# Twelve instead of six shared steps ahead of the expert blocks in the last sparse layer

## The reference, cut to what matters

```
x = x + 0.5 * L3_ffn(layernorm(x))
x = x + L3_attn(layernorm(x))
x = x + 0.5 * L3_ffn(layernorm(x))

L3_ffn(x):                                     # 8 experts of 176, two per token; shared part of 704
    probs  = softmax(x @ W_router.T)           # [T, 8]
    rw,sel = top_k(probs, 2)
    sh     = (silu(x@Ws_gate) * (x@Ws_up)) @ Ws_down
    shared = sh * sigmoid(x @ W_sgate.T)
    eo[e]  = (silu(x@We_gate[e]) * (x@We_up[e])) @ We_down[e]
    return shared + sum_e combine[:, e] * eo[e]
```

## Time and profile before

| | |
|---|---|
| median of 3 runs | 3719.99 us (3718.23 to 3720.12) |
| the profiled execution, its own time | 3711.44 us |
| its span, first to last instruction | 3709.6 us |
| mean granted TensorE clock | 0.895 of full |
| PE busy / DVE busy / ACT busy / POOL busy | 3038.5 / 2194.1 / 1489.1 / 1115.9 us |

### The profile page before, as it was taken

How to read it: one execution, slowest core, us unless ns; L and a number is a source line. 1 busy time by engine, 2 the same in 40 slices (tenths; PEclk the granted TensorE clock), 3 DMA queues, 4 the chain that set the end, 5 groups by cost and what they waited for, 6 DMA issues and landing times.

```text
span 3709.6 us, 56721 instructions
## 1 busy us (share of the span) xinstructions
PE 3038.5 (82%) x19164; PEld 2581.3 (70%) x19164; DVE 2194.1 (59%) x5486; ACT 1489.1 (40%) x3661; POOL 1115.9 (30%) x1085
## 2 busy tenths in 40 slices
PE   4597999999999955889479796948888685986698
PEld 2476888888888834769458594836666574975597
DVE  3644555555555546556473667657778667655664
ACT  2124443444444321233532344437677344424342
POOL 2002222222222220054350544541111455431543
PEclk8798999999999967999779997859899887998899
DMA  2002111111111110033110243520000263311232
GB/s 77 1 0 92 64 48 63 47 63 47 65 45 66 47 46 0 7 95 111 46 34 0 88 124 94 135 74 2 1 1 1 70 160 115 105 56 46 85 107 74
DMA packets 115095, 222.71 MB, mean 60 GB/s; under 512 B 17313, under 2 KB 66945, under 8 KB 110273
## 3 DMA queue, kind: packets, MB, share of 16 engines
q1 hardware_dynamic: 80754, 149.30, 12.5%
q0 software_dynamic: 21472, 58.36, 6.1%
q10 hardware_dynamic: 12672, 12.58, 1.0%
HBM read 172.74 MB, written 47.85 MB: 59 GB/s over the span
## 4 chain that ended last, share of the span: by engine, by line
PE 37%; issue 29%; DVE 16%; POOL 8%; ACT 5%; DMA 4%; SPq 0%; DVEq 0%; ACTq 0%; POOLq 0%
PE bank L502 9%; PE bank L504 9%; PE bank L503 9%; POOL HWL L1737 3%; POOL YG L1498 2%; POOL KL L1753 2%; PE bank L1081 2%; PE bank L1997 1%; DVE ST L528 1%; PE bank L2013 1%; ACT XN L552 1%; PE bank L1103 1%; DMA YG<-dyo,POSI 1%; DMA MXG<-dxn,IDX 1%; DVE SG L749 1%
## 5 line engine op out<-in xcount | busy, mean ns | idle before, releaser
L1488 POOL DMA_INDIRECT MXG<-dxn,IDX x250 | 237.5, 950 | 319.2 <-PE bank L1081 163.8
L1753 POOL TENSOR_TENSOR QL<-QG,QH 128x512 fp32r<-128x512 f32 x64 | 83.0, 1296 | 729.7 <-ACT QH L1645 729.7
L1498 POOL DMA_INDIRECT YG<-dyo,POSI x192 | 190.1, 990 | 218.2 <-DMA dyo<-YS 110.7
L1683 DVE TENSOR_TENSOR X<-bank,X 128x512 f32<-128x512 f32 x128 | 82.5, 686 | 226.9 <-PE bank L504 226.9
L622 PE MATMUL bank<-TAB,XN 128*128 128x128 f32 x320 | 72.8, 385 | 168.1 <-ACT XN L552 127.7
L1480 POOL TENSOR_TENSOR MWL<-RAW,MWH 128x608 fp32r<-128x608 f32 (+2 forms) x118 | 182.1, 1553 | 79.2 <-ACT MWH L1184 73.0
L1478 POOL CAST MWH<-RAW 128x608 fp32r<-128x608 f32 (+2 forms) x78 | 55.0, 705 | 467.6 <-DVE X L884 369.1
L622 PEld LDWEIGHTS bank<-TAB,XN 128*128 128x128 f32 x320 | 52.2, 196 | 181.7 <-ACT XN L552 114.3
L502 PE MATMUL bank<-MWH,GH 128*128 x500 | 173.9, 348 | 0.0
L2174 DVE COPY PT<-bank 128x384 f32<-128x384 f32 x256 | 131.8, 551 | 64.0 <-PE bank L1997 55.3
L502 PE MATMUL bank<-MWH,SHH 128*128 128x256 f32 x352 | 110.1, 313 | 72.2 <-DVE SHL L1357 57.9
(11 more groups left out here) (439 smaller groups left out, 11201.2 us busy)
## 6 DMA issues: line engine op xcount, KB each, us to landing
dyo<-YS SPq DMA_DIRECT2D x250, 128.0 KB
RAW<-in_wheads SPq DMA_DIRECT2D x68, 320.0 KB, 3.0
RAW<-in_eL SPq DMA_DIRECT2D x64, 304.0 KB, 2.9
BB<-dgates SPq DMA_DIRECT2D x17, 1024.0 KB, 4.5
GB<-dgates SPq DMA_DIRECT2D x17, 1024.0 KB, 6.5
dxn<-XN ACTq DMA_DIRECT2D x16, 512.0 KB, 4.3
RAW<-in_eL SPq DMA_DIRECT2D x32, 256.0 KB, 2.7
RAW<-in_sL SPq DMA_DIRECT2D x18, 384.0 KB, 3.9
```

Source lines behind the costliest of these rows:

```text
L1488: nc.gpsimd.indirect_dma_start(MXG[:, n % XGS, :], None, dxn, bass.IndirectOffsetOnAxis(ap=IDX[:, b:b + 1], axis=0)).then_inc(x_in[n % XGS ...
L1498: nc.gpsimd.indirect_dma_start(YG[:, i % YGS, :], None, dyo[0:m.blocks * P, :], bass.IndirectOffsetOnAxis(ap=POSI[:, c * NT + t:c * NT + t ...
L1753: nc.gpsimd.tensor_tensor(lo[:, :], src[:, :], f32(hi[:, :]), ALU.subtract).then_inc(qk_ready, 1)
```

## The change

`pre` of the layer goes from 1 to 2, so `early` = 12 and `late` = 12 in stages A and B; everything derived from them moves too (`pieces_by`, `added_in`, `slot_of`). The four DVE chunks stay at steps 2 to 5. The products of chunks 2 and 3 (`moe_inverse`) move from behind the loop into steps 6 and 7, and `moe_index` from step 5 to step 7. The two other sparse layers have `early` = 6 before and after, and their order is the same as before.

```diff
-    'L3': Sparse(E=L3_E, F=L3_I, J=6, pre=1, act=ACT.Silu, gated=True, router=3),
+    'L3': Sparse(E=L3_E, F=L3_I, J=6, pre=2, act=ACT.Silu, gated=True, router=3),
@@ moe_tensor
                 if s == 5:
                     moe_inverse(pe, st, 1)
+                if s in (6, 7):
+                    moe_inverse(pe, st, s - 4)
                 if s:
                     shared_down(pe, st, s - 1)
-            moe_inverse(pe, st, 2)
+            if m.early == 6:
+                moe_inverse(pe, st, 2)
             shared_down(pe, st, m.early - 1)
-            moe_inverse(pe, st, 3)
+            if m.early == 6:
+                moe_inverse(pe, st, 3)
             warm(24, 1)
@@ moe_vector
                 if s == 5:
                     moe_hot(dve, st, 3)
+                if s == (5 if m.early == 6 else 7):
                     moe_index(dve, st)
             shared_add(dve, st, m.pre - 1)
```

## The result

The changed kernel takes 3711.32 us (median of 20 runs, 3695.37 to 3727.34), the kernel before 3722.66 us (20 runs, 3707.52 to 3734.78). The ratio is 0.9963, with a 95% interval of 0.9948 to 0.9979: 0.37% or some 13.8 us faster. The profiled execution took 3698.85 us, with a span of 3697.0 and a granted clock of 0.894, against 3711.44, 3709.6 and 0.895 before: 12.6 us less of both.

A forecast was written before the change was run, and what follows sets the result against it. PE was taken to set the pace in the late steps, DVE during the routing. A +12.5 - 24.7 = -12.2 and B +20.9 - 24.7 = -3.8, together -16.0 from 3720.0: 3704 us, range 3697 to 3714.

The forecast's parts named there:

- Stage B, early: Stage B up to its first turn: six more early steps and bare warm matmuls bring that turn 23.3 us later.
- The give-back by rows that lie ready: Start of B's block pipeline: gathered rows already there give back 2.4 us (bounds 0 and 3).
- The late phase: Late steps of both stages: six steps fewer, -25.4 us, plus 0.7 of combine waits, so -24.7 each.
- Rival 2: Late phases: the gathers set the pace, four us more in each stage, total 3712 us; chance 0.08.
- Stage A, early: Stage A up to its first turn: DVE sooner but POOL ending last, so that turn comes 12.5 us later.
- The relief of DVE: A's routing: fewer POOL pieces collide with DVE, so SHL of step 5 comes 8.7 us sooner.
- the price of the pieces that stay: A's routing: each of six POOL pieces still beside DVE's work ahead of SHL of step 5 costs 1.0 us.
- From there PE goes at its pace: Early steps behind the down of step 6, both stages: PE waits for nothing, 4.23 us per step.
- rival 4: Moved early steps run at half clock, up to 4.2 us more each; all twelve give 3754 us; chance 0.05.
- Rival 3: More relief in A's routing (lock's worst, 4.3 us more) and a cleaner block start: -22, 3698 us; chance 0.09.
- the lock at its worst: A's routing: DVE and GpSimd block each other 1.6 us per piece, relief 13 us and not 8.7.
- Rival 5: Nothing gained: IDX is hidden, but warm matmuls and POOL take its place; 3719 us or so; chance 0.05.

The follow-up runs named there:

- e2: Changed kernel with the last two inverse products and `moe_index` back behind the loop, twelve early steps kept; 3789.57 us in a single run.
- e11: Changed kernel with `pre=3`: 18 shared steps ahead of the blocks and six late; 3782.69 us in one run (kernel before: median 3783.85 on that chip).
- e4: Changed kernel with one combine tile per late slot, first try; 3780.61 us in a single run.
- e6: Changed kernel, unchanged, profiled and timed again; 3712.53 us (12 runs) against 3727.82 of the kernel before, ratio 0.9961.
- e9: Changed kernel with one combine tile per late slot, second try on another chip; late phases 58.07 and 60.11 us, no total given.
- e3: Changed kernel without the 24 warm matmuls ahead of this layer's blocks; 3789.12 us in a single run.
- e8: Changed kernel with stage A's first four gathers issued by POOL ahead of the last two subtractions; 3707.92 us.
- e7: Changed kernel with only pieces 4 and 5 beside A's routing, the other 16 at steps 6 to 11; 3718.91 us in one run.
- e1: Changed kernel with `pieces_by` at its old pace, all 22 pieces done by step 6; 3784.46 us in a single run.
- e10: Changed kernel with light routing, no warm matmuls and one tile per late slot together; 3754.52 us (10 runs), ratio to the kernel before 0.9922.
- e12: The kernel before, unchanged, profiled once more on a fourth chip; the single profiled runs of that kernel took 3714.24 and 3722.47 us.

## Why the prediction was right, and where it was off

**Stage B, early: right.** From the first up (3478.80) to the first turn (3547.13) there are 68.3 us, against 45.2 before: +23.1, predicted +23.3. No gather holds the first turn, the warm matmuls are bare (2.63 us by their starts), and the ups of steps 8 to 11 follow at 4.23. The give-back by rows that lie ready is right too: the first turned hidden comes 5.25 us after the first turn (predicted 5.3, before 7.7), and from the first turn to the first late up there are 83.67 us against 86.07 before, -2.4 as predicted. But the 2.4 are not the dripping gathers alone, as the prediction had it. In all three profiles of the kernel before the clock is at half over the first blocks of B (this is the first of them), and so it is in e2; in no profile of B with the index cast early is it:

```profile
3534.65:3538.06 3.41, 3.41 (x14) 3.34 (x13) 1.19 (x3) 1.08 (x3) 2.50 (x4) 0.50 0.33 101
```

PE is busy all of these 3.41 us, so up to 1.7 of the 2.4 us (an estimate: half of them) are clock. The number was right, its cause only in part.

**The late phase: right.** First late up to last add: 57.17 us in A and 57.40 in B against 82.18 and 82.94, so -25.0 and -25.5, predicted -24.7. The downs of slots 4, 5 and 7 wait 1.07, 0.82 and 1.53 in A (predicted 0.7, 1.1, 1.9), and in B slot 4 waits 2.30, slot 6 0.22 and slot 7 1.21: 3.4 and 3.7 us, predicted 3.7. Rival 2 (the gathers set the pace, four us more a stage) falls for twelve late steps, and e11 shows that six late steps are past the point where it holds.

**Stage A, early: the terms that were mis-sized.** The first turn is 78.73 us behind the stage's start, against 63.34 before, so +15.4, predicted +12.5. In the sum the two terms that follow are off, and one that was left out:

- The relief of DVE was put at 8.7 us (14.7 us of collisions ahead of SHL of step 5, less six pieces at 1.0). It is 7.2 between the two first profiles, 7.8 between those of the other group (51.6 to 43.8), and 7.5 in the means (52.03 to 44.57). The 14.7 was right: the stretched operations add up to 14.7 to 15.3 us. The step that failed is the price of the pieces that stay. The six cost 7.5 us and not 6.0, 1.2 each: an average over 18 pieces was put on six that come in pairs, right beside the one-hots, where a pair costs 2.4 us. In the old order 16 pieces and not 14 or so start ahead of that SHL, at 0.9 each. The one piece beside the last chunk costs 1.2 us in place of 1.0 as well.
- "From there PE goes at its pace" left out the clock: the down of step 6 waits 2.44 us, and it and the start of the next up run at half clock (0.55 over 3149.50 to 3153.30), 1.6 us. e4, e6 and e9 have the same at the same place, behind a wait of 2.43 us. In e3 and e8 it comes one step sooner, behind a wait of 1.61 us of the down of step 5, and the down of step 6 then waits 0.9 us only: another place, no better block mark. In e7 neither wait is over 0.8 us, and the clock stays 1.00 there. So rival 4 came true for one step, and the moved steps behind it ran at 1.00. The down that waits 2.81 us in the kernel before lies at half clock too (its first matmul has 0.58 us instead of 0.39) and could have been read as a warning.
- The rest was 0.2 to 0.4 us better than assumed: the last piece is through POOL in 1.51 us, as estimated, and the first turn comes 2.84 us after the first gather (2.8).

Over the stage: +15.4 - 0.1 in the blocks (85.36 us from first turn to first late up against 85.5) - 25.0 = -9.7, predicted -12.2; by the means over profiles -10.0. For B -3.6 by the means (-4.8 between the two profiles), predicted -3.8.

**The sum.** -13.6 by the stages and -13.8 by the ratio, predicted -16.0. The 2.2 to 2.4 us between are stage A's two terms, 1.2 to 1.5 and 1.6 us, of which the rest of A and the late phases gave some 0.5 to 0.7 back. The absolute 3704 us leant on three runs of the kernel before (3719.99); over 20 runs its median is 3722.66, and the changed kernel's 3711.32. Of the 7.3 us between forecast and measurement 2.7 are this base, 2.2 the size of the change by the ratio, and 2.4 that the two medians differ by 11.3 us where the ratio gives 13.8.

**Rival 3, and the rule weighed against the trace.** The relief came out under the forecast and not over it, so the lock at its worst (13 us) is not seen at the new pace. The Trainium skill (SBUF — State Buffer, "Who interferes with whom") says which instructions block each other, and e7 agrees: with no piece beside it AHOT takes 0.56 and BHOT 1.23 us in stage A, as in stage B, and with a pair 1.74 and 2.42. What it costs in the mean was 0.9 us a piece in the old order and 1.2 at the new pace, where the forecast had 1.0 and the lock at its worst 1.6.

**Rival 5** falls by e2: with the index back behind the steps, 5 to 8 of the 13.6 us are lost. One can put the gain so: the steps moved at equal price; what they brought is the cover of IDX and its gathers (3.9 to 4.5 us in B, 1.3 to 3.4 in A) and DVE's relief in A, of which e1 takes away 6 to 8 us up to the last block; against them stand the bare warm matmuls and the slower entry of A.

## What to carry to other kernels

Work that one engine could do anywhere (here shared products on PE) is worth moving only for what it covers: find the stall, list what each moved step still has to wait for, and stop at the point where the phase it leaves becomes bound by something else (here 32 gathers of 1.26 us; six late steps were too few). A pacing function that is derived from a count is part of the change when the count changes: in stage A the new pace of the pieces is worth 6 to 8 of the 10.0 us gained. What remains beside a bottleneck is to be priced by what it then lies beside, and not by the average of before. And where unchanged code varies by more than the change does, compare marks inside the changed stage, over more than one profile of each kernel.

## What the hardware showed that was not expected

**Stops that nothing in the trace releases.** On the two chips on which the kernel before takes 3770 and 3784 us, all seven kernels with twelve or more early steps have long stops in the late phase, and none of the seven profiles from the other chips has one. ACT waits with its SiLU, and the profile can only say "remote" or "issue". The first fence is ACT's timeline in e3, first in another sparse layer and then in stage B; the second is PE's, with the down that waits for it in the end:

```profile
2246.36 0.60 ACT L1170 ACTIVATE SGS<-bank 128x512 f32<-128x512 f32 x1 [12.29 <-remote]
...
3741.20 0.60 ACT L1170 ACTIVATE SGS<-bank 128x512 f32<-128x512 f32 x1 [13.63 <-remote]
```

```profile
3743.96 0.58 PE L502 MATMUL bank<-MWH,SHH 128*128 128x256 f32 x1 [5.25 <-DVE SHL L1362]
```

In e10 the stop is 8.89 us; in e9 PE stands 3.10 and 3.98 us for it. They make the late phases of e1, e2 and e3 some 10 us longer than those of the second chip (66.9 to 69.0 against 56 to 59). The packets that load instructions do not fall together with them (in e3 none starts from 3712.5 to 3749.6 us, and ACT stands from 3727.6 to 3741.2). No profile of the kernel before was taken on these chips (e12 was to be one, and ran on a quicker chip). But the stops are not made by the combines that now come early, for they are all over the run. Ahead of stage A, in code that is the same in every kernel here, ACT and PE have 17 to 24 such stops of over 1 us in each of these seven profiles, 6 to 9 of them over 5 us (the longest 11 to 14 us), and none in the other seven. Stage A begins at 3141 to 3172 us in the seven and at 3097 to 3123 in the others. So they belong to these chips, or to what ran on them then. What causes them stays open, and so does how many the kernel before has in its own late phases there.

**The cost of an engine's silence in clock.** A wait of PE of 2.44 us inside dense work was followed by some 3.4 us at half clock, 1.6 us lost; one of 1.01 us in stage B (3523.00) was followed by none, nor was one of 1.47 us at the same place in e2. Kernels with the same order took the loss one step sooner behind a wait of 1.61 us, so the length of a wait alone does not tell where it comes.
